# A graph network on one core: source rows of the last 16 of 56 chunks gathered in the first layer, from a table of rows of 130 words

## What is computed

```python
def _L0_gnn_ref(x, edge_index, W, b, ln_gamma, ln_beta):
    h = x @ W                                        # 50000 x 128
    src, dst = edges and one loop for each node
    deg = segment_sum(ones, dst);  dinv = rsqrt(deg)
    out = segment_sum(h[src] * (dinv[src] * dinv[dst])[:, None], dst) + b
    return relu(layernorm(out) * ln_gamma + ln_beta)
x = layernorm(x + _L0(x))     # this layer, called gcn in the kernel
x = layernorm(x + _L1(x))     # three attention layers on the same edges (conv)
x = layernorm(x + _L2(x))     # mean of the neighbours (sage), then batch norm
x = layernorm(x + _L3(x))     # attention with edge rows (angle)
```

## Time and profile before

| | us |
|---|---|
| median of 3 runs (7023.27 to 7031.01) | 7026.21 |
| the profiled execution | 7027.23 |
| its span, first to last instruction | 7025.3 |
| setup, until its last gather starts | 538.5 |
| setup, until the first layer begins | 551.5 |
| the first layer, until POOL's last gather | 1591 |
| conv, sage, batch norm, angle | from about 1709 |

### The profile page before, as it was taken

The page is one execution under the profiler, slowest core; times in us unless marked ns, Lnnn a source line. Parts: engine busy times, 40 slices in busy tenths (PEclk is TensorE's granted clock), DMA queues, the critical chain, the costliest instruction groups (busy, mean ns, idle before and its releaser), DMA issues. The chain is left out here.

```text
span 7025.3 us, 129182 instructions
## 1 busy us (share of the span) xinstructions
PE 4875.6 (69%) x27083; PEld 3611.4 (51%) x27083; DVE 5733.4 (82%) x28646; ACT 4768.1 (68%) x13748; POOL 4470.3 (64%) x4380
## 2 busy tenths in 40 slices
PE   4104333332999987999948888884997659888882
PEld 1002222221877766777736666653664547666661
DVE  9814777775999987999949999995775877999996
ACT  0002888884888885888948888883553656888884
POOL 7776777772655526555537777744774445777774
PEclk8555555555999998999979999996998989999995
DMA  3333555552555534555524555544664873444441
GB/s 100 99 104 83 133 131 128 130 132 84 178 185 178 190 138 140 185 185 177 176 86 152 170 170 170 169 147 130 205 203 148 295 269 120 148 147 147 147 145 44
DMA packets 507778, 1065.66 MB, mean 152 GB/s; under 512 B 225329, under 2 KB 259196, under 8 KB 506998
## 3 DMA queue, kind: packets, MB, share of 16 engines
q1 hardware_dynamic: 373618, 811.78, 35.3%
q0 software_dynamic: 133504, 247.46, 13.2%
HBM read 559.18 MB, written 500.53 MB: 151 GB/s over the span
## 5 line engine op out<-in xcount | busy, mean ns | idle before, releaser
L1801 POOL DMA_INDIRECT xs<-tab,rec x1176 | 1187.9, 1010 | 737.0 <-issue 325.1
L1891 ACT ACTIVATE z<-p_a 128x512 f32<-128x512 f32 x1176 | 696.4, 592 | 307.1 <-PE p_a L1734 299.3
L1885 ACT ACTIVATE st<-xs,cb 128x128 f32<-128x128 f32 x2352 | 807.5, 395 | 0.5 <-DVE cg L1530 0.5
L1836 PE MATMUL p_a<-w_all,xt 128*128 128x256 f32 x2352 | 735.5, 395 | 19.9 <-ACT xt L1876 16.4
L1804 POOL DMA_INDIRECT xd<-tab,rec x616 | 621.0, 1008 | 187.8 <-issue 179.9
L1839 PE MATMUL p_y<-w_all,xt 128*128 128x258 f32 x2352 | 725.0, 390 | 21.1 <-DVE cA L1956 20.5
L1991 DVE SCALAR_TENSOR_TENSOR st<-st,cg 128x128 f32<-128x128 f32 x2352 | 711.5, 342 | 6.8 <-ACT st L1885 4.6
L1956 DVE CUSTOM_DVE_ANT_0 junk<-p_y,xs 128x129 f32<-128x129 f32 x2352 | 579.9, 283 | 53.5 <-PE p_y L1839 51.1
L1738 PE MATMUL p_m<-w_all,z 128*128 128x128 f32 x2352 | 580.0, 329 | 0.0
L999 PE MATMUL p_m<-b_rows,ones_bf 3*128 3x512 bf16 x224 | 100.1, 447 | 688.8 <-ACT z L1042 688.8
L1734 PE MATMUL p_a<-ident,st 128*128 128x128 f32 x2352 | 465.2, 280 | 145.1 <-DVE st L1991 144.9
(11 more groups left out here) (756 smaller groups left out, 16246.7 us busy)
## 6 DMA issues: line engine op xcount, KB each, us to landing
states<-st SPq DMA_DIRECT2D x168, 910.0 KB
own<-tab SPq DMA_DIRECT2D x168, 448.0 KB
tab<-o SPq DMA_DIRECT2D x168, 448.0 KB
runs<-run SPq DMA_DIRECT2D x112, 448.0 KB, 2.9
tab<-out SPq DMA_DIRECT2D x112, 448.0 KB
x<-tab SPq DMA_DIRECT2D x112, 448.0 KB, 4.3
angles<-st SPq DMA_DIRECT2D x56, 532.0 KB, 2.9
xsrc<-got SPq DMA_DIRECT2D x56, 448.0 KB
```

The lines of the kernel that those rows point to most:

```text
L1801: pool.indirect_dma_start(xs[:, i, j, 0:D], None, table, bass.IndirectOffsetOnAxis(ap=rec[:, i, SRC, j : j + 1], axis=0)).then_inc(got_in[ ...
L1836: ins = pe.matmul(p_a[two(own_c, own_i)][:, 2 * D : 4 * D], xt[:, two(c, i), D : 2 * D], k.w_own[:], start=True, stop=True)
L1885: ins = act.activation(state_of(r, j)[:, h, :], xs[:, c.slot(UB), j, 0:D], ACT.Copy, scale=co.b[:, c.slot(2), h, j : j + 1])
L1891: act.activation(z[:, c.slot(RING), j, :], p_a[two(c, j)][:], ACT.Copy).then_inc(st_copied, 1)
```

## The change

The setup gathers source rows and fills `xsrc` for the first 40 chunks only (`k.early`, 5 turns of 8; L442's loop and SP's with it). In the first layer these 40 chunks go as before, but the part of `xsrc` and the words of `info` now land in one tile `both`, rows of 130 words, so that the load of `xsrc` writes runs of 512 bytes.

A new DRAM table `x_info` has 50176 rows of 130 words (520 bytes): the row of `x` and the two words of `info`. It is filled in 32 pieces (`PIECES`) of 1568 rows, one piece with the loads of each of the first 32 chunks: one transfer of 1568 runs of 512 bytes and one of 1568 runs of 8 bytes, DRAM to DRAM, on SP's queue. From chunk 40 on POOL gathers rows of `x_info` by SRC in place of `info`, still 14 gathers per chunk, and SP loads no `xsrc`. POOL waits once, before the gathers of chunk 40, for all 64 transfers (`x_ready`). As the code of a chunk now depends on its number, the hardware loop of this stage runs for the turns 1 and 2 only (`cut` = 3), and the turns 3 to 6 are written out.

```diff
-def turns(eng, n, body):
-
+def turns(eng, n, body, cut=None):
+    cut = n - 1 if cut is None else min(cut, n - 1)
     body(0)
-    if n > 2:
-        with eng.Fori(1, n - 1) as t:
+    if cut > 1:
+        with eng.Fori(1, cut) as t:
             body(t)
-    if n > 1:
-        body(n - 1)
+    for t in range(max(cut, 1), n):
+        body(t)
...
+class Span:
+    def __init__(self, blocks):
+        self.TN, self.NB = blocks, blocks * UB
+PIECES = 32
...
+        self.early = Span(max(1, min(self.TN * 5 // 7, self.TN - 1)))
...
-                    ch = Chunk(k, t, u, EAHEAD)
+                    ch = Chunk(early, t, u, EAHEAD)
                     if ch.there:
                         wait(sp, got_in[ch.slot(UB)], ch.use(UB) * 16 * J)
                         sp.dma_start(idx[:, ch.slot(UB), :], src[:, ch.n, :]).then_inc(idx_in[ch.slot(UB)], 16)
-                    ch = Chunk(k, t, u)
+                    ch = Chunk(early, t, u)
                     if ch.there:
                         wait(sp, got_in[ch.slot(UB)], (ch.use(UB) + 1) * 16 * J)
                         sp.dma_start(rows(k.xsrc)[:, ch.n, :], got[:, ch.slot(UB)].rearrange("p j d -> p (j d)")).then_inc(put_out[ch.slot(UB)], 16)
-                walk(k, sp, one, EAHEAD, 0)
+                walk(early, sp, one, EAHEAD, 0)
...
-                    ch, i = Chunk(k, t, u), u % UB
+                    ch, i = Chunk(early, t, u), u % UB
...
-                walk(k, pool, one, 0, 0)
+                walk(early, pool, one, 0, 0)
...
+                        if bring:
+                            bring(sp, c)
...
-                walk(k, sp, one, LEAD, DRAIN)
+                walk(k, sp, one, LEAD, DRAIN, cut)
...
-        n = Flow(k, c, 2, 2, 1)
+        n = Flow(k, c, 1, 2, 1)
         first, second = LogNorm(k, c, 0), LogNormTwice(k, c, 1)
-        xs, own = n.x
-        where = sb("where", [P, UB, J, 2], I32)
+        own, = n.x
+        both = sb("both", [P, UB, J, D + 2])
+        xs, where = both[:, :, :, 0:D], both[:, :, :, D : D + 2]
+        xs_in, x_ready = [sem(f"xs_in{u}") for u in range(UB)], sem("x_ready")
...
+        plain = lambda c: not isinstance(c.n, int) or c.n < k.early.NB
+        def pieces(table):
+            return table.rearrange("(q r) d -> q r d", q=PIECES)
+        def bring(sp, c):
+            if plain(c):
+                sp.dma_start(xs[:, c.slot(UB)], rows(k.xsrc)[:, c.n, :].rearrange("p (j d) -> p j d", j=J)).then_inc(xs_in[c.slot(UB)], 16)
+            if not isinstance(c.n, int) or c.n < PIECES:
+                sp.dma_start(pieces(k.x_info)[c.n, :, 0:D], pieces(A["x"])[c.n]).then_inc(x_ready, 16)
+                with nc.allow_non_contiguous_dma(reason="two words beside each row"):
+                    sp.dma_start(pieces(k.x_info)[c.n, :, D : D + 2], pieces(k.info.bitcast(F32))[c.n]).then_inc(x_ready, 16)
+        def fetch(pool, c):
+            i = c.slot(UB)
+            wait(pool, n.rec_in[i], (c.use(UB) + 1) * 16, n.passed)
+            if not plain(c) and c.n == k.early.NB:
+                pool.wait_ge(x_ready, PIECES * 32)
+            for j in range(J):
+                mine = bass.IndirectOffsetOnAxis(ap=n.rec[:, i, NODE, j : j + 1], axis=0)
+                source = bass.IndirectOffsetOnAxis(ap=n.rec[:, i, SRC, j : j + 1], axis=0)
+                pool.indirect_dma_start(own[:, i, j, :], None, A["x"], mine).then_inc(n.got[i], 16)
+                if plain(c):
+                    pool.indirect_dma_start(where[:, i, j, :], None, k.info.bitcast(F32), source).then_inc(n.got[i], 16)
+                else:
+                    pool.indirect_dma_start(both[:, i, j, :], None, k.x_info, source).then_inc(n.got[i], 16)
         def weigh(act, c):
             i = c.slot(UB)
-            n.wait_loaded(act, c)
+            if plain(c):
+                act.wait_ge(xs_in[i], (c.use(UB) + 1) * 16)
...
-        n.run([(xs, k.xsrc)], [(own, A["x"], NODE), (where, k.info, SRC)], [k.res, k.tab[1]], lambda c: [R(summed, c)], [k.w_skip],
+        n.n_got = 2
+        cut = max(1, min(k.early.TN, PIECES // UB) - (LEAD + UB - 1) // UB)
+        n.run([], [], [k.res, k.tab[1]], lambda c: [R(summed, c)], [k.w_skip],
...
+    k.x_info = dram("x_info", [k.NR, D + 2])
```

More of the change, by code:

```diff
@@ L206, in land, with walk @@
         self.eng.wait_ge(self.sems[mark[0]], mark[1])
-def walk(k, eng, one, lead, drain):
+def walk(k, eng, one, lead, drain, cut=None):
     for u in range(-lead, 0):
@@ L216, in body @@
             one(t, u)
-    turns(eng, k.TN, body)
+    turns(eng, k.TN, body, cut)
     for u in range(UB, UB + drain):
@@ L333, in setup @@
     NB, COLS, T = k.NB, k.COLS, k.T
+    early = k.early
     with ExitStack() as c:
@@ L415, in _ @@
                 for u in range(UB):
-                    sp.wait_ge(put_out[u], k.TN * 16)
+                    sp.wait_ge(put_out[u], early.TN * 16)
             @b.gpsimd
@@ L935, in run @@
     def run(self, ins, gathers, outs, srcs, weights, dve_stages, act_stages, pool_stages, prep=False, pe_stages=(), sp_stages=(),
-            begin=None, sp_end=None, sp_begin=None, pe_begin=None, sp_after=None):
+            begin=None, sp_end=None, sp_begin=None, pe_begin=None, sp_after=None, fetch=None, bring=None, cut=None):
         k, nc, n_src = self.k, self.nc, self.n_src
-        self.n_loaded, self.n_got = len(ins), len(gathers)
+        self.n_loaded = len(ins)
+        self.n_got = self.n_got or len(gathers)
         chunk = lambda t, u, lag=0: Chunk(k, t, u, lag)
@@ L1022, in _ @@
                     pe_begin(pe)
-                walk(k, pe, one, LEAD, DRAIN)
+                walk(k, pe, one, LEAD, DRAIN, cut)
             @b.scalar
@@ L1056, in one, with gather @@
                                 carry_product(c, g)
-                walk(k, act, one, LEAD, DRAIN)
+                walk(k, act, one, LEAD, DRAIN, cut)
             @b.gpsimd
             def _(pool):
-                def fetch(pool, c):
+                def gather(pool, c):
                     i = c.slot(UB)
@@ L1068, in fetch @@
                                                     bass.IndirectOffsetOnAxis(ap=self.rec[:, i, f, j : j + 1], axis=0)).then_inc(self.got[i], 16)
-                stages = ([(AHEAD, fetch)] if gathers else []) + list(pool_stages)
-                walk(k, pool, lambda t, u: run_stages(pool, stages, t, u), LEAD, DRAIN)
+                stages = ([(AHEAD, fetch or gather)] if fetch or gathers else []) + list(pool_stages)
+                walk(k, pool, lambda t, u: run_stages(pool, stages, t, u), LEAD, DRAIN, cut)
             @b.vector
@@ L1085, in one @@
                             step.end()
-                walk(k, dve, one, LEAD, DRAIN)
+                walk(k, dve, one, LEAD, DRAIN, cut)
 class RowNorm:
@@ L1358, in weigh @@
             for j in range(J):
-                act.activation(R(run, c)[:, j, :], xs[:, i, j, :], ACT.Copy, scale=where[:].bitcast(F32)[:, i, j, 1:2])
+                act.activation(R(run, c)[:, j, :], xs[:, i, j, :], ACT.Copy, scale=where[:, i, j, 1:2])
                 ins = act.activation(R(summed, c)[:, j, :], own[:, i, j, :], ACT.Copy, scale=n.field(c, OWN2)[:, j : j + 1])
@@ L1379, in keep @@
             with nc.allow_non_contiguous_dma(reason="one of two words"):
-                sp.dma_start(k.meta[:, c.n, SRC, :], where[:, c.slot(UB), :, 0]).then_inc(src_out[c.slot(UB)], 16)
+                sp.dma_start(k.meta[:, c.n, SRC, :], where[:, c.slot(UB), :, 0].bitcast(I32)).then_inc(src_out[c.slot(UB)], 16)
         def kept(sp):
@@ L1420, in gcn @@
               [], prep=True, sp_stages=[(3, keep)], begin=begin, sp_end=kept,
-              pe_begin=side.tensor, sp_after={-4: side.bring, UB - 1: side.put_away})
+              pe_begin=side.tensor, sp_after={-4: side.bring, UB - 1: side.put_away}, fetch=fetch, bring=bring, cut=cut)
         head, mine, hint, o, ot, z = [sb(x, s) for x, s in (("head", [P, D]), ("mine", [P, D]), ("hint", [P, 2]), ("o", [P, D]),
```

## The result

The changed kernel takes 6906.91 us (median of 4 runs, 6905.34 to 6911.79) against 7024.74 us before (4 runs, 7019.71 to 7031.01): a ratio of 0.9832, interval 0.982 to 0.9845. It is **faster by 118 us**, or 1.7%. The profiled execution took 6907.68 us, its span is 6906.0 us; against the profiled execution of before (7027.23) that is 119.6 us less. The forecast was 6906.

What follows compares the result with a forecast made beforehand. POOL's gathers, about 1.25 us each, were taken to bound the setup and first layer. 7027.2 - 139.8 (setup) + 12 (start) + 7 (build) gave 6906 us; own range 6886 to 6940, whole range 6882 to 7160.

Steps and rivals of the forecast that it cites:

- Setup, -139.8: Setup: 280 gathers instead of 392 on POOL, so its end comes 139.8 us earlier.
- The cover: Setup's end: DVE's last copies at 390.4 us against SP's write of meta at 401.7, 11 us remaining.
- Start, +12: First layer's start: two pieces ahead of fifteen small loads lengthen POOL's wait by 12 us, bounds 7 and 16.
- Build, +7: First layer, chunks 0 to 31: table building mostly hidden under POOL at 16.2 us a chunk; 7 us put in.
- half of an overflow at 18.6 us a chunk: Build's upper end: 0.4 us a chunk over POOL's 18.18, 14 us in 32 chunks; half taken, 7 us.
- rec of a chunk is issued a chunk ahead of its gathers: First layer: rec goes out a chunk early and lands in 1.8 us, or 5.8 to 9.6 queued, inside 18.
- POOL waiting for rec in every chunk: Sign of being wrong, first layer: POOL waits for rec each chunk; chunks over 19 us until the 32nd.
- SP's 327.5 us of waiting for ACT: First layer's steady stretch: SP waits 327.5 us for ACT's last operation of a chunk, read as SP having room.
- 130-word gathers, 0: First layer's last 16 chunks: gathers of 130 words cost no more than 944 ns; bounds nothing or 34 us.
- The sum: Whole kernel: 7027.2 - 139.8 + 12 + 7 = 6906.4, stated as 6906 us.
- the rows' price: Rival, table build: rows at multiples of 520 bytes add 4.7 to 9.4 us a piece; 7076 to 7236 us; chance 0.25.
- The words' price in full: Rival, table build: words cost 4.7 to 7.0 us a piece; 6917 to 6995 us, middle 6956; chance 0.18.

Runs made afterwards that it cites:

- the kernel without pieces: Changed kernel with all 56 chunks gathered in the setup and no table built; 8761.77 us against 8752.63 before, ratio 1.0007.
- the wide table's kernel: Kernel with all 56 chunks gathered early, only row pieces copied, table rows 1024 bytes apart; 8717.71 us against 8765.58 before, one execution.

## Why the prediction was right, step by step

- **Setup, -139.8:** right, measured 139.8 at the first rec. The cover held, at 12.4 us.
- **Start, +12:** measured +15.5 at POOL, +14.8 at PE. The cause was right (pieces gone from ahead of the small loads, start back to 9 us), its size just under the upper bound of 16. The parts were off: rows 5.55 us, not 3.1; words 2.7, not 2.35. Together two pieces cost 12.5 us on the other chips and 14.8 on the first, so the parts don't add up (11.1 + 5.4 = 16.5), and 13.0 of the 14.8 pass at SP's issues, before the small loads are in the queue in which the forecast let them wait.
- **Build, +7:** measured +14.9 over the whole steady stretch, just over the upper bound of 14. It was taken as half of an overflow at 18.6 us a chunk; the DMA work was 17.5 us, below POOL's 18.18, and POOL still lost 0.6 us a chunk. Two steps failed. One is that the build is hidden as long as the sum is below POOL's pace: the sum was below it and the build was not hidden, and on another chip a sum above the chunk's time (1.14 x 22.2 = 25.4 us) lengthened no chunk. The other is that rec of a chunk is issued a chunk ahead of its gathers: it goes out when ACT frees the slot, in the case shown 1.5 us before POOL was free and too late for its 1.8 us of landing. The prediction named POOL waiting for rec in every chunk as a sign of being wrong; it did so in about half of them beside the build. Why ACT is later there is argued, not shown. I had read SP's 327.5 us of waiting for ACT as room; it was a sign of how little room rec has.
- **130-word gathers, 0:** right, 944 ns.
- **The sum:** these terms give 139.8 - 15 - 15 = 110, not 121. That the time is 6907 and not 6917 is the 7.4 us from the untouched conv and 1 us behind it. Neither was in the forecast, so its meeting the median to 1 us is luck; its terms were 11 us off. (Its own range begins at 6886, where 7027.2 - 139.8 is 6887; nothing hangs on it.)
- **The rivals:** the rows' price is real but 3.0 us, a third to two thirds of what was feared, which leaves a chunk at 18.8 us, far from the 21.9 at which the gain would be gone. The words' price in full (4.7 to 7.0 us) did not come. The Trainium skill's rule on transfers below 512 bytes ("DMA: Bandwidth & Descriptors", Specifications) points the right way, since 1568 times 8 bytes cost about as much at the start (2.7 us) as 1568 times 512 aligned bytes (2.55), and more than half as much in SP's queue (1.0 and 1.8). But a scattered pair is cheaper than the 3.0 ns a word that I had read from meta: 1.7 ns a pair at the start.

## What was not expected

**One program, two limits.** On the other chips the setup of the kernel without pieces ends not with POOL but with DVE. The last table and the gathers (first and last start):

```profile
L654 DVE COPY rec<-tmp x1: 366/366/366, 816.7 to 816.7; 128x392 f32<-128x392 f32 x1
```

```profile
L454 POOL DMA_INDIRECT got<-in_x,idx x392: 941/947/1793, 7.3 to 529.4; - x196
```

Its timeline at 202 us, and DVE's waits from 30 to 530 us (total us, times, longest):

```profile
201.78 0.94 POOL L454 DMA_INDIRECT got<-in_x,idx  x1 [0.30 <-issue]
202.19 0.25 DVE L569 TENSOR_SCALAR hi<-iota_h,hi 128x128 bf16<-128x128 f16 x1 [1.08 <-issue]
203.03 0.95 POOL L454 DMA_INDIRECT got<-in_x,idx  x1 [0.30 <-issue]
203.58 0.47 DVE L570 TENSOR_SCALAR lo<-iota_h,lo 128x392 bf16<-128x392 f16 x1 [1.14 <-issue]
```

```profile
DVE lo L570 <- issue: 189.1, 170, 1.8
DVE hi L569 <- issue: 185.4, 169, 5.3
```

DVE gets through about one instruction per gather and waits 1.1 us in between for nothing that the profile shows. The stages say the same, while the gathers run and once they are over:

```profile
100.00:200.00 100.00, 12.91 (x37) 4.72 (x38) 23.49 (x76) 0.00 (x0) 69.15 (x74) 1.00 0.33 97
600.00:700.00 100.00, 26.65 (x99) 10.51 (x98) 94.23 (x299) 3.00 (x3) 0.00 (x0) 0.60 0.00 0
```

DVE is busy 23.49 of 100 us in the one and 94.23 in the other. On the first chip, in the kernel before, the same stretch is the other way round:

```profile
100.00:200.00 100.00, 66.77 (x256) 26.66 (x255) 100.00 (x510) 0.00 (x0) 80.50 (x65) 0.76 0.27 83
```

There DVE is busy all the time, with 510 instructions, and POOL's instructions take 80.50 / 65 = 1.24 us each, against 69.15 / 74 = 0.93 on the other chip. It looks as if the two engines were in each other's way on both chips, and as if POOL's gathers paid on the one and DVE's operations on the other; that is argued from these stretches, and the traces don't tell why it falls out differently. Taking gathers away helps here too, by another path: DVE is held for less long. On one chip its last table comes at 815.7 us with 392 gathers (the wide table's kernel), 679.3 with 280 and 614.3 with 224, which is 1.22 and 1.16 us per gather taken away, about a gather with its gap. That is why 32 early chunks took their 65 us in full. The forecast's argument for the setup (POOL last, DVE done 11 us before) would have been false on these chips, and its number nearly right, 136 us. What makes them differ was not found.

In the first layer of these chips POOL has slack. Its waits in the kernel without pieces, 600 to 2000 us, of which the longest, 299.0, is the end of the setup:

```profile
POOL in L1385 <- DMA rec<-meta: 620.7, 31, 299.0
```

That leaves 322 us in 30 waits, and fits that rows or words alone, and 16 large pieces, cost nothing that a time can tell. The cost of the build's chunks and of the start is thus shown for the first chip by its trace alone; moving the pieces there (about 14 us, an estimate from the start's 22.9 and 8.9) was not measured.

**A gather's price doesn't depend on its row.** In the first layer 2, 128 and 130 words take 944 ns and 0.30 us to the next. In the setup of the first chip, beside a busy DVE, it is 1.24 us, so what stands beside a gather can matter where its row doesn't.

## What to carry to other kernels

Gathers with one index per partition cost POOL 1.25 us each here, whether they brought 2 or 130 words, so take them out of a stretch in which POOL (or, behind it, DVE) sets the end, and put the words into a row that is fetched anyway. A copy into rows 520 bytes apart cost 2.2 to 2.5 times one into rows 1024 bytes apart. Place such a copy in the queue behind the small loads that the next engine waits for: what is queued behind it is late to be issued, not only to land. Don't read a DMA share as room: at 0.93 a chunk lost 0.6 us of 18.2, though the sum fitted under the pacing engine, and at 1.14 on another chip, where POOL had slack, it lost nothing. Look instead at how far ahead of its need each small load is issued, and which engine's slot holds it back.
